# Gated linear-scan mixer with a routed feed-forward: batch loop written out, a fifth plane added by DMA, small work moved in the engines' orders

## Chip, cores and metric

The kernel runs on one core of a Trainium2 chip. The metric is device time of one execution in microseconds. Before the change three runs took 678.12, 679.08 and 682.12 us; the median is 679.08 us. The five engines of the core each run a program of their own and meet only at semaphores: PE (TensorE: matrix products and transposes), DVE (VectorE), ACT (ScalarE), POOL (GpSimd) and SP (SyncE, which here only issues DMAs). POOL issues DMAs too.

## What is computed

The input x is 8 batches of 1024 tokens of 256 features. In short:

```python
x = x + layernorm(attn(layernorm(x)))
x = x + layernorm(ffn(layernorm(x)))

# attn: 4 mixers m, each token weighs its best two
g, v, d = z @ Wg[m] + bg[m], z @ Wv[m] + bv[m], z @ Wd[m] + bd[m]
a = 0.001 + 0.998 * sigmoid(d)
h[t] = a[t] * h[t-1] + sigmoid(g[t]) * tanh(v[t])     # scan along the 1024 tokens
attn = sum over m of comb[:, m] * h_m                  # comb: softmax of the two best gate logits

# ffn: each batch is sent to one of 8 experts
z = layernorm(x) * ln_g + ln_b
probs = softmax(batchnorm(mean over tokens of z) @ Wr + br); e = argmax(probs)
ffn = (relu(z @ W_down[e] + b_down[e]) @ W_up[e] + b_up[e]) * probs[e]
```

## The kernel before, in words

**Tiling.** A batch is 1024 tokens. The mixers work on the transposed batch (features on partitions): 4 mixers times 2 halves of 128 features give 8 *planes* of 128 x 1024. A plane needs three projections (gate, decay, value) for two chunks of 512 tokens, so a batch has 48 *products*, numbered i = 0 to 47 in the code (plane i // 6). One product is 6 matmuls of 128 x 512 (weights and input are each split into a high and a low half-precision part; three of the four cross terms, over two halves of the contraction). Three PSUM banks take turns, so product i waits until ACT has read product i-3 (`main_read`). ACT's `evacuate` applies the sigmoid or tanh and writes the plane to one of four slots (`gate_s`, `decay_s`) or to `hid`.

**DVE's part of a plane** is `multiply` (gate times value, L932), `scan` (L914) and `weigh` (times the token's weight of that mixer, L926).

**Sum over mixers.** Plane p and plane p+2 are the same features of successive mixers. POOL's `add_plane(p)` (L486) is a DMA that adds plane p to plane p+2 in SBUF; it is issued for p = 0 to 3, one after the other, so that planes 4 and 5 hold the sum of three mixers. PE's `turn_plane` (L1389) then transposes planes 4, 5, 6, 7 (`TURNED`) back to token rows, 8 transposes of 128 x 128 each, and sums what is left in PSUM (`ps_aux`, seen by tokens as `ps_tok`).

**What follows the sum, for the batch before (`pv`), while the products of the present batch run:** on DVE `a_moments` (statistics of the turned rows), `residual`, `t_moments`, `scale_t`; on ACT `normalise_t` (L640); on PE `turn_u` (L1326); on ACT `high_u`; on PE `route`; on DVE `low_u` (L959), `route_logits`, `route_pick` (L978); SP reads the expert's index and copies its weights (`load_expert`); on PE `down` (L1448); `high_h`, `low_h`, PE's `up`; on DVE `y_moments`, `scale_y` (L1015); on ACT `scale_rows` (L663, eight rows, in pairs ahead of products 43 to 46); on DVE `finish` (L1022, adds the residual) and SP's `store`.

**For the batch after (`nx`):** `x_moments`, `normalise_x`, `high_rows_x` and `low_rows_x` (split), two DMA transposes by SP (`move_x`, L400, which wait for `plane_added[1]`), PE's `gates`, DVE's `rank_mixers`, ACT's `shares`, DVE's `weights_of` (`comb`), PE's `turn_weights` (L1354), DVE's `copy_weights` (L904), and SP's saving and loading of the weights (`save_comb`, `load_comb`).

**Order.** There is no scheduler. Each engine's program is written by hand: PE and ACT in three functions (`run_first`, `run`, `last`) that walk over the 48 products and put other work ahead of a given i; DVE in a list of calls per batch. `iterations` (L232) runs batch 0 as `run_first`, batches 1 to 6 in a loop of the hardware with two batches in its body (three passes), and batch 7 as `last`, which cuts the batch into two chunks. An engine does its work strictly in its order, so a wait holds up all that is written behind it.

**First batch.** SP loads weights; ACT casts each weight matrix to its high part (`high_matrix`, L537), DVE makes the low part (`low_matrix`, L830). `hidden_bias` (L1489, L1492) are 33 narrow matmuls ahead of product 15 that need `prepare_router` (ends in L1085) and other constants. Some `prepare_` calls on DVE ready the experts' weights.

## Time and profile before

| | |
|---|---|
| profiled execution, time | 678.97 us |
| its span, first to last instruction | 677.2 us |
| PE busy | 618.5 us, 91% |
| DVE busy | 587.4 us, 87% |
| ACT busy | 461.1 us, 68% |
| POOL busy | 99.7 us, 15% |
| mean granted clock of PE | 0.974 |

Matmuls are pipelined; a row's duration is longer than the step from one to the next (a 128 x 512 matmul shows 0.38 us and the next begins 0.216 us later at full clock, so that a product steps by 1.296 us). In a timeline row the first number is the start in us from the start of the span, the second the duration (of the whole merged group where the count behind the x is above 1), and the bracket tells how long the engine sat idle before it and what ended that.

### The profile page before, as it was taken

What the parts mean: (1) busy time and instruction counts of PE and PEld (TensorE: products, weight loads), DVE (VectorE), ACT (ScalarE), POOL (GpSimd) and SP (SyncE); (2) the same over time, 40 slices, a digit from 0 to 9 for tenths busy, and PEclk for the clock granted to TensorE, in tenths of its full rate; (3) what the DMA queues carried; (4) which work ended last, traced back from release to release, by engine and by line L of the source; (5) the groups of instructions that cost most, each with busy time, mean ns of one, the idle gap of its engine ahead of it and who ended that gap; (6) DMA issues with size and microseconds to landing.
All of it is one profiled execution on the core that took longest, in us unless ns stands there. A gap on an engine that the chain in (4) does not pass through costs nothing. (4 is left out here: it accounts for less than half of the span.)

```text
span 677.2 us, 10435 instructions
## 1 busy us (share of the span) xinstructions
PE 618.5 (91%) x3314; PEld 318.4 (47%) x3314; DVE 587.4 (87%) x1094; ACT 461.1 (68%) x791; POOL 99.7 (15%) x101
## 2 busy tenths in 40 slices
PE   3989999999999989999998989999998999899673
PEld 2454454445545535445544535445544554444431
DVE  6799599999899987999899987999899988889866
ACT  3728655896579675896579675896669775877404
POOL 2002011302121101302121101202030102112011
PEclk9979999999999999999999999999999999999687
DMA  8651736154712736054621737045631735211003
GB/s 224 153 187 32 156 62 237 26 111 78 253 60 54 141 101 219 1 106 93 233 80 43 144 100 228 0 96 104 209 104 43 130 99 179 44 31 32 0 22 115
DMA packets 74627, 73.27 MB, mean 108 GB/s; under 512 B 36134, under 2 KB 66122, under 8 KB 74570
## 3 DMA queue, kind: packets, MB, share of 16 engines
q1 hardware_dynamic: 69676, 56.30, 28.8%
q0 software_dynamic: 4896, 16.26, 12.9%
q8 instruction: 32, 0.52, 0.3%
q14 instruction: 23, 0.19, 0.1%
HBM read 38.85 MB, written 8.52 MB: 70 GB/s over the span
## 5 line engine op out<-in xcount | busy, mean ns | idle before, releaser
L1375 PE MATMUL ps_main<-xh,w_hi 128*128 128x512 f16 x768 | 292.5, 381 | 6.9 <-issue 5.7
L1375 PE MATMUL ps_main<-xh,w_lo 128*128 128x512 f16 x768 | 292.4, 381 | 0.0
L1375 PE MATMUL ps_main<-xl,w_hi 128*128 128x512 f16 x768 | 292.3, 381 | 0.0
L914 DVE TENSOR_TENSOR_SCAN hid<-decay_s,hid 128x1024 f32<-128x1024 f32 (+1 forms) x64 | 138.2, 2159 | 6.6
L581 ACT ACTIVATE hid<-ps_main,vecs 128x512 f32<-128x512 f32 x128 | 88.9, 695 | 60.5 <-PE ps_main L1375 60.1
L581 ACT ACTIVATE decay_s<-ps_main,vecs 128x512 f32<-128x512 f32 x128 | 88.9, 695 | 59.1 <-PE ps_main L1375 57.9
L1375 PEld LDWEIGHTS ps_main<-xh,w_hi 128*128 128x128 f16 x768 | 76.1, 99 | 94.6 <-issue 7.8
L581 ACT ACTIVATE gate_s<-ps_main,vecs 128x512 f32<-128x512 f32 x128 | 88.6, 692 | 44.8 <-PE ps_main L1375 43.8
L1375 PEld LDWEIGHTS ps_main<-xl,w_hi 128*128 128x128 f16 x768 | 75.4, 98 | 91.6 <-issue 1.7
L1375 PEld LDWEIGHTS ps_main<-xh,w_lo 128*128 128x128 f16 x768 | 75.3, 98 | 85.7 <-issue 1.1
L932 DVE TENSOR_TENSOR hid<-gate_s,hid 128x1024 f32<-128x1024 f32 (+1 forms) x72 | 79.5, 1105 | 6.5 <-ACT hid L581 6.0
L926 DVE TENSOR_TENSOR hid<-hid,comb_all 128x1024 f32<-128x1024 f32 (+1 forms) x72 | 79.7, 1107 | 2.8
L587 ACT ACTIVATE decay_s<-decay_s 128x1024 f32<-128x1024 f32 (+1 forms) x72 | 69.6, 967 | 0.0
L486 POOL DMA_DIRECT2D hid<-hid x34 | 30.0, 882 | 245.6 <-DVE hid L926 170.8
L468 POOL TENSOR_TENSOR root_a<-root_in_a,neg_half 128x8 f32<-128x8 f32 (+1 forms) x9 | 19.0, 2111 | 151.8 <-DVE root_in_a L816 151.8
L1326 PE MATMUL ps_aux<-ident,normed 128*128 128x128 f32 x136 | 19.5, 302 | 23.4 <-ACT normed L640 13.2
L1389 PE MATMUL ps_aux<-ident,hid 128*128 128x128 f32 x264 | 32.9, 285 | 3.3 <-DVE hid L926 2.2
L1389 PEld LDWEIGHTS ps_aux<-ident,hid 128*128 128x128 f32 x264 | 31.3, 148 | 5.8 <-DVE hid L926 2.8
L640 ACT ACTIVATE normed<-resid,shift_t,root_t 128x256 f32<-128x256 f32 x60 | 30.5, 595 | 4.2 <-DVE shift_t L823 4.2
L594 ACT ACTIVATE u_split<-ps_aux 128x512 f16<-128x512 f32 x32 | 18.9, 600 | 19.0 <-PE ps_aux L1411 17.7
L808 DVE BATCH_NORM_STATS2 stats_a<-ps_aux 128x6 f32<-128x256 f32 x64 | 22.1, 419 | 10.5 <-PE ps_aux L1389 10.5
L1326 PEld LDWEIGHTS ps_aux<-ident,normed 128*128 128x128 f32 x136 | 16.9, 155 | 27.8 <-ACT normed L640 17.1
(152 smaller groups left out, 606.9 us busy)
## 6 DMA issues: line engine op xcount, KB each, us to landing
comb_all<-comb_dram SPq DMA_DIRECT2D x32, 512.0 KB, 5.1
hid<-hid POOLq DMA_DIRECT2D x28, 512.0 KB, 4.6
x_in<-in_L_attn_x SPq DMA_DIRECT2D x16, 512.0 KB, 7.5
resid<-in_L_attn_x SPq DMA_DIRECT2D x8, 1024.0 KB, 6.1
out<-resid SPq DMA_DIRECT2D x7, 1024.0 KB, 5.5
expert<-experts SPq DMA_DIRECT2D x8, 192.5 KB, 2.2
hid<-hid POOLq DMA_DIRECT2D x6, 256.0 KB, 3.3
w_stage<-in_L_attn_Wg SPq DMA_DIRECT2D x4, 256.0 KB, 3.9
```

The costliest lines, as they stand in the source:

```text
L468: pool.tensor_tensor(root[key][:, span(c)], root_in[key][:, span(c)], neg_half[:, span(c)], ALU.pow).then_inc(rooted, units(c))
L486: pool.dma_start(hid[:, p + KT, tokens(c)], hid[:, p, tokens(c)], accum_op=ALU.add).then_inc(plane_added[p], 16)
L581: act.activation(dst, ps_main[:, i % BANKS], ACT.Tanh if kind == VALUE else ACT.Sigmoid, bias=vecs[:, col:col + 1], scale=Q_W).then_inc(ma ...
L587: act.activation(d, d, ACT.Copy, bias=0.001, scale=0.998).then_inc(decay_ready, 1)
L640: ins = act.activation(out[:, t], rows[:, t], ACT.Identity, bias=shift[key][:, t:t + 1], scale=root[key][:, t:t + 1])
L808: ins = dve.bn_stats(out=stats[key][:, t], in_=rows(t))
L914: dve.tensor_tensor_scan(states(pc), staged(decay_s, pc, pc.c), states(pc), start, ALU.mult, ALU.add).then_inc(scanned, 1)
L926: dve.tensor_tensor(src, src, comb_all[:, m, tokens(pc.c)], ALU.mult).then_inc(weighed, 1)
L932: dve.tensor_tensor(v, staged(gate_s, pc, pc.c), v, ALU.mult).then_inc(input_ready, 1)
L1326: ins = pe.transpose(ps_aux[:, KT * cc + k, tile(t % (T // C))], normed[:, t, k * P:(k + 1) * P], ident[:])
L1375: ins = pe.matmul(ps_main[:, i % BANKS], w[:, 3 * m + kind, k, half * P:(half + 1) * P], v[:, bt.par, span(c), k], start=(n == 0), stop=(n ...
L1389: ins = pe.matmul(ps_tok[:, t, k * P:(k + 1) * P], hid[:, p, tile(t)], ident[:], is_transpose=True, start=(p == (LATE_TURNED if c else TUR ...
```

## The change

The hardware loop goes: `iterations` now calls `run` six times, with batch numbers known when the program is built. POOL issues a fifth addition, plane 4 to plane 6, and PE turns only planes 5, 6 and 7; it does so one product later (i = 5). Small work changes its place. In steady batches: PE turns the weights ahead of product 45 and not behind 47; ACT's `shares` stands ahead of product 43, before the wait for `y_scaled`, and not ahead of 44; on DVE `weights_of` moves ahead of plane 6, `finish` and then `copy_weights` stand between plane 6 and plane 7, and `route_logits` stands before `low_u`. In the first batch ACT, DVE and PE take the casts, splits, gates and preparations in another order.

```diff
-    TURNED = (4, 5, 6, 7)
+    TURNED = (5, 6, 7)
...
-        def iterations(eng, run_first, run, last):
+        def iterations(run_first, run, last):
...
-            with eng.Fori(0, B // 2 - 1) as j:
-                for r in (1, 2):
-                    run(turn(j, r), turn(j, r + 1), turn(j, r - 1))
+            for n in range(1, B - 1):
+                run(turn(n // 2, n % 2), turn((n + 1) // 2, (n + 1) % 2), turn((n - 1) // 2, (n - 1) % 2))
...
# POOL, run
                 power("y", y_root_in, y_root, pv)
+                add_plane(bt, 4)
# POOL, last
                 add_plane(bt, 3, 0)
+                add_plane(bt, 4, 0)
...
# ACT, run_first
+                        high_matrix(0, VALUE)
                         high_x(bt, 0)
-                        high_matrix(0, VALUE)
+                    if i == 1:
+                        high_gate_weights()
                         mixer_high(1)
                         high_x(bt, 1)
-                    if i == 3:
-                        high_gate_weights()
+                    if i == 4:
+                        mixer_high(2)
                     if i == 6:
-                        mixer_high(2)
-                    if i == 7:
+                        mixer_high(3)
+                    if i == 9:
                         shares(bt)
-                        mixer_high(3)
-                    if i == 21:
+                    if i == 25:
                         normalise_x(nx, tiles(0))
-                    if i == 25:
+                    if i == 26:
                         normalise_x(nx, tiles(1))
...
# ACT, run
                     if i == 23:
                         normalise_x(nx, tiles(0))
-                    if i == 24:
                         router_sigmoids(pv)
...
                     if i == 43:
+                        shares(nx)
                         act.wait_ge(xh_moved, 16 * nx.n)
                         act.wait_ge(xl_moved, 16 * nx.n)
                         act.wait_ge(y_scaled, pv.n + 1)
                         scale_rows(pv, (0, 1), normed)
                     if i == 44:
-                        shares(nx)
                         scale_rows(pv, (2, 3), normed)
...
# DVE, ahead of the first batch
             x_moments(first, 0)
+            scale_x(first, 0)
+            normalise("x", x_in, x_scaled, x_normed, first, 0)
             low_matrix(0, GATE)
-            scale_x(first, 0)
             low_matrix(0, DECAY)
-            normalise("x", x_in, x_scaled, x_normed, first, 0)
+            low_matrix(0, VALUE)
             x_moments(first, 1)
+            copy_vecs()
             low_x(first, 0)
-            copy_vecs()
-            low_matrix(0, VALUE)
...
# DVE, run_first
                 mixer_low(1)
+                prepare_router(prep)
+                mixer_low(2)
+                rank_mixers(bt)
                 set_ones()
-                rank_mixers(bt)
                 weights_of(bt)
-                mixer_low(2)
-                mixer_low(3)
                 copy_weights(bt, True)
-                prepare_up_biases(prep)
-                prepare_router(prep)
                 prepare_down(prep, 0)
                 multiply(bt, pcs[0])
...
# DVE, run
+                route_logits(pv)
                 low_u(pv)
-                route_logits(pv)
                 route_pick(pv)
...
                 scale_y(pv)
+                weights_of(nx)
                 multiply(bt, pcs[6])
                 scan(bt, pcs[6])
                 weigh(bt, pcs[6])
-                weights_of(nx)
+                finish(pv)
                 copy_weights(nx, False)
                 multiply(bt, pcs[7])
                 scan(bt, pcs[7])
                 weigh(bt, pcs[7])
-                finish(pv)
...
# PE, run_first
-                    if i == 5:
+                    if i == 3:
                         first_gates(bt)
-                    if i == 8:
+                    if i == 11:
                         turn_weights(bt)
...
# PE, run
-                    if i == 4:
-                        turn_planes(pv, (4, 5, 6, 7))
+                    if i == 5:
+                        turn_planes(pv, (5, 6, 7))
...
+                    if i == 45:
+                        turn_weights(nx)
                     product(bt, i, bank, False)
-                turn_weights(nx)
```

The engines' orders at the places that matter. First PE, from the end of the loop's body: the rows before show the turning of the weights, the jump back to the loop's start, and (word for word the first rows behind it) the next product.

```order
L1354 MATMUL ps_misc<-ident,comb 32x128 [waits comb_ready]
L238 REGISTER_ALU
L238 COMPARE_AND_BRANCH
L1375 MATMUL ps_main<-xh,w_hi 128x512 [waits main_read,xl_moved,xh_moved]
L1375 MATMUL ps_main<-xh,w_lo 128x512
```

In the program after the change no L238 row stands on PE at all; the weights' transpose has moved three products up. The turning of the planes in a steady batch, with the names of the semaphores that each plane waits for (`plane_added4` is the new addition), now reads:

```order
L1391 MATMUL ps_aux<-ident,hid 128x128 [waits plane_added3,weighed,y_normed]
L1391 MATMUL ps_aux<-ident,hid 128x128 x7
L1391 MATMUL ps_aux<-ident,hid 128x128 [waits plane_added4,weighed]
L1391 MATMUL ps_aux<-ident,hid 128x128 x7
L1391 MATMUL ps_aux<-ident,hid 128x128 [waits weighed]
L1391 MATMUL ps_aux<-ident,hid 128x128 x7
```

Before, four such pairs stood there, the first for plane 4. On DVE the end of a steady batch, from `scale_y` to the first statistics of the next batch, read before:

```order
L1015 TENSOR_TENSOR shift_y<-shift_y,shift_a 128x8 [waits out_link]
L930 REGISTER_ALU
L932 TENSOR_TENSOR hid<-gate_s,hid 128x1024 [waits main_read]
L914 SCALAR_TENSOR_TENSOR hid<-decay_s,hid 128x1024 [waits input_ready,decay_ready]
L926 TENSOR_TENSOR hid<-hid,comb_all 128x1024 [waits comb_loaded3,scanned]
L897 TENSOR_TENSOR comb<-share,chosen 128x8x4 [waits share_ready]
L904 COPY comb_rows<-ps_misc 32x128 [waits comb_saved,comb_turned]
L930 REGISTER_ALU
L932 TENSOR_TENSOR hid<-gate_s,hid 128x1024 [waits main_read]
L914 SCALAR_TENSOR_TENSOR hid<-decay_s,hid 128x1024 [waits input_ready,decay_ready]
L926 TENSOR_TENSOR hid<-hid,comb_all 128x1024 [waits scanned]
L1022 TENSOR_TENSOR resid<-normed,resid 128x2048 [waits y_normed]
```

After the change the same stretch of DVE is (line numbers are two higher):

```order
L1017 TENSOR_TENSOR shift_y<-shift_y,shift_a 128x8 [waits out_link]
L899 TENSOR_TENSOR comb<-share,chosen 128x8x4 [waits share_ready]
L934 TENSOR_TENSOR hid<-gate_s,hid 128x1024 [waits main_read]
L916 SCALAR_TENSOR_TENSOR hid<-decay_s,hid 128x1024 [waits input_ready,decay_ready]
L928 TENSOR_TENSOR hid<-hid,comb_all 128x1024 [waits comb_loaded3,scanned]
L1024 TENSOR_TENSOR resid<-normed,resid 128x2048 [waits y_normed]
L906 COPY comb_rows<-ps_misc 32x128 [waits comb_saved,comb_turned]
L934 TENSOR_TENSOR hid<-gate_s,hid 128x1024 [waits main_read]
L916 SCALAR_TENSOR_TENSOR hid<-decay_s,hid 128x1024 [waits input_ready,decay_ready]
L928 TENSOR_TENSOR hid<-hid,comb_all 128x1024 [waits scanned]
```

The weights' product has moved ahead of plane 6, where it waits for ACT's `share`, and the addition of the residual ahead of plane 7, where it waits for all of ACT's scaled rows.

## Rows read from the trace of the kernel before

**Rows 1.** The page, part 1: busy us (share of the span) and instructions by engine.

```profile
PE 618.5 (91%) x3314; PEld 318.4 (47%) x3314; DVE 587.4 (87%) x1094; ACT 461.1 (68%) x791; POOL 99.7 (15%) x101
```

**Rows 2.** Timeline of PE: the weights' transposes that end batches 1 and 6.

```profile
169.81 0.27 PE L1354 MATMUL ps_misc<-ident,comb 128*32 128x128 f32 x1
...
551.56 0.27 PE L1354 MATMUL ps_misc<-ident,comb 128*32 128x128 f32 x1
```

**Rows 3.** Busy time by stretch (start:end length, engines, clock, DMA): batches 2 and 3.

```profile
170.00:245.10 75.10, 73.22 (x402) 37.16 (x400) 68.81 (x121) 56.75 (x98) 11.96 (x8) 1.00 0.44 116
245.10:323.30 78.20, 73.43 (x404) 37.45 (x403) 68.84 (x121) 56.91 (x99) 11.96 (x8) 1.00 0.44 111
```

**Rows 4.** Waits in batch 3 (engine, line, what ended it: us, times, longest).

```profile
PE ps_main L1375 <- issue: 2.8, 1, 2.8
```

**Rows 5.** Timeline, start of batch 2: plane 7 weighed, planes turned, residual added.

```profile
174.82 1.23 DVE L926 TENSOR_TENSOR hid<-hid,comb_all 128x1024 f32<-128x1024 f32 x1
175.10 3.66 PE L1389 MATMUL ps_aux<-ident,hid 128*128 128x128 f32 x32
175.96 2.28 DVE L1022 TENSOR_TENSOR resid<-normed,resid 128x2048 f32<-128x2048 f32 x1
```

**Rows 6.** Timeline, batch 2: from DVE's scale to ACT's rows and PE's transposes.

```profile
197.76 0.17 DVE L823 SCALAR_TENSOR_TENSOR shift_t<-moments_t,root_t 128x8 f32<-128x8 f32 x1
...
199.03 1.09 ACT L640 ACTIVATE normed<-resid,shift_t,root_t 128x256 f32<-128x256 f32 x2
...
203.13 1.97 PE L1326 MATMUL ps_aux<-ident,normed 128*128 128x128 f32 x16 [1.07 <-ACT normed L640]
```

**Rows 7.** Timeline, batch 2: low parts, router and expert.

```profile
207.53 2.48 DVE L959 TENSOR_TENSOR u_split<-ps_aux,u_split 128x512 f16<-128x512 f32 x4
...
211.70 0.20 DVE L978 RECIPROCAL r<-r 128x8 f32<-128x8 f32 x1 [0.64 <-ACT r L600]
...
214.76 1.90 PE L1448 MATMUL ps_aux<-u_split,expert 128*128 128x512 f16 x8 [0.32 <-DMA expert<-experts]
```

**Rows 8.** Timeline, end of batch 2: scale, first and last scaled rows, plane 6.

```profile
238.87 0.17 DVE L1015 TENSOR_TENSOR shift_y<-shift_y,shift_a 128x8 f32<-128x8 f32 x1
...
239.48 1.02 ACT L663 ACTIVATE normed<-ps_aux,shift_y,root_y 128x256 f32<-128x256 f32 x2
...
242.62 1.23 DVE L926 TENSOR_TENSOR hid<-hid,comb_all 128x1024 f32<-128x1024 f32 x1
...
244.02 1.08 ACT L663 ACTIVATE normed<-ps_aux,shift_y,root_y 128x256 f32<-128x256 f32 x2
```

**Rows 9.** Timeline: an addition's issue, and SP's transpose that waits for it.

```profile
217.89 0.86 POOL L486 DMA_DIRECT2D hid<-hid  x1 [8.77 <-DVE hid L926]
...
223.11 1.76 SPq L400 DMA_TRANSPOSE xh<-normed  x1
```

**Rows 10.** POOL's line of the 34 additions: time from issue to landing.

```profile
DMA to landing us min/median/max: 3.2/4.5/6.4
```

**Rows 11.** Timeline, first batch on PE, ACT and DVE.

```profile
26.84 1.66 ACT L537 ACTIVATE w_hi<-w_stage 128x512 f16<-128x512 f32 x3
...
29.33 3.69 DVE L830 SCALAR_TENSOR_TENSOR w_lo<-w_stage,w_hi 128x512 f16<-128x512 f32 x6
29.49 0.29 PE L1354 MATMUL ps_misc<-ident,comb 128*32 128x128 f32 x1 [1.64 <-DVE comb L897]
...
40.94 0.36 PE L1489 MATMUL ps_misc<-z_wr,ones 128*128 128x8 f32 x2 [2.10 <-DVE z_wr L1085]
...
47.49 0.59 PE L1375 MATMUL ps_main<-xh,w_hi 128*128 128x512 f16 x1
```

**Rows 12.** Busy time by stretch in the narrow matmuls: clock is the last but two.

```profile
41.80:42.20 0.40, 0.40 (x4) 0.40 (x3) 0.40 (x2) 0.00 (x0) 0.00 (x0) 0.50 1.03 341
```

**Rows 13.** Timeline of PE: the last planes of batch 0, turned in batch 1.

```profile
102.33 1.09 PE L1389 MATMUL ps_aux<-ident,hid 128*128 128x128 f32 x8 [0.99 <-DVE hid L926]
```

**Rows 14.** Timeline of PE, last batch: the wait for ACT's rows.

```profile
579.23 0.98 PE L1326 MATMUL ps_aux<-ident,normed 128*128 128x128 f32 x7 [3.19 <-ACT normed L640]
```

More of the change, by code:

```diff
@@ L193, in mixer_kernel @@
         weighed = sem("weighed")
-        plane_added = [sem(f"plane_added{p}") for p in range(4)]
+        plane_added = [sem(f"plane_added{p}") for p in range(5)]
         add_go = sem("add_go")
@@ L441, in last @@
                 sp.wait_ge(out_stored, 16 * (B + 2 * C) + 1)
-            iterations(sp, run_first, run, last)
+            iterations(run_first, run, last)
         @block.gpsimd
@@ L526, in last @@
                 power("y", y_root_in, y_root, bt, 1)
-            iterations(pool, run_first, run, last)
+            iterations(run_first, run, last)
         @block.scalar
@@ L782, in last @@
                 scale_late_rows(bt, 1)
-            iterations(act, run_first, run, last)
+            iterations(run_first, run, last)
         @block.vector
@@ L1314, in last @@
                 finish_late(bt, 1)
-            iterations(dve, run_first, run, last)
+            iterations(run_first, run, last)
         @block.tensor
@@ L1567, in last @@
                 up(bt, 1)
[L1569 removed]
+            iterations(run_first, run, last)
 _INS = ["L0_attn_x", "L0_attn_Wg", "L0_attn_bg", "L0_attn_Wv", "L0_attn_bv", "L0_attn_Wd", "L0_attn_bd",
```

28 lines of the change are left out of this document (15 added, 13 removed).

## Prediction, made before the changed kernel ran

> **What bounds the kernel now.** I read the page's busy times first, then the trace batch by batch. PE is busy for 618.5 of 677.2 us, DVE for 587.4 [rows 1]: both are close to the bound, and a share of the whole cannot say which sets the pace. The transposes of the weights close each batch on PE and serve as a clock: batch 1 closes at 169.81, batch 6 at 551.56 [rows 2]. By stretch, batch 2 lasts 75.10 us and batch 3 lasts 78.20 with the same work [rows 3]; batch 4 repeats the one and batch 5 the other. Inside 75.1 us PE is busy for 73.2 and DVE for 68.8: **in a steady batch PE sets the pace, and DVE has a few us of slack**. The long batches are the two that begin behind a jump back of the loop, and there PE waits 2.8 us at a product for "issue", that is for nothing that a semaphore shows [rows 4].
>
> I measure inside a steady batch from the end of PE's turning of the planes, T. In batch 2 that is 175.10 + 3.66 = 178.76 [rows 5].
>
> **The change, part by part.**
>
> *Loop written out.* The two jumps back go. Each costs 78.2 - 75.1 = 3.1 us [rows 3], and since PE is the bound the whole of it goes: **-6.2**. Below that the gain is nothing if written-out code brings stalls of its own. Batches 1 and 2 are code run for the first time, in a straight line, and show no such wait in 75.1 us [rows 3], so I take the full price.
> The Trainium skill, "Runtime: NRT & Kernel Launch", section "Instruction fetch mechanics", says that straight code is fetched ahead and that a taken branch out of the fetched window stalls. The trace agrees, with 2.8 us.
>
> *Three planes turned, not four.* 32 transposes take 3.66 us [rows 5], so eight fewer are **-0.92** per batch on PE.
>
> *The turning one product later.* PE loses nothing by it, but DVE's chain behind it starts later against the products. That chain ends with `scale_t` at 197.93, T + 19.17; ACT takes it up at 199.03, 1.10 later, because it came there only then, by the products [rows 6]. A product steps by 1.296 us, so now one product fewer lies between T and ACT's arrival: ACT is 1.30 earlier, uses up the 1.10 and waits 0.20. PE's wait at the transposes grows from 1.07 by that: **+0.20**.
>
> *`route_logits` before `low_u`.* The index is known 2.48 us earlier [rows 7], DVE's wait of 0.64 for the sigmoids is covered by `low_u`, and PE's wait of 0.32 for the expert's weights goes: **-0.35** (0.3 to 0.5 over the batches).
>
> A steady batch so takes 75.1 - 0.92 + 0.20 - 0.35 = 74.05 us.
>
> *Can DVE follow?* `scale_y` ended at 239.04, T + 60.28. PE and ACT now are 1.3 + 0.35 - 0.20 = 1.45 earlier against T. Two waits are new. `weights_of` waits for ACT's `share`; ACT, which began its rows at 239.48, now comes at T + 59.3 and is held until `scale_y`. `finish` waits for all eight rows, 5.6 us of ACT's time (239.48 to 245.10), and then takes 2.28 [rows 5] ahead of plane 7, which takes 4.8 like plane 6 (239.04 to 243.85) [rows 8]. If DVE is no earlier than before, rows end at T + 65.9, `finish` at 68.2, plane 7 at 73.3. If it keeps the 0.64 and some smaller waits it is rid of, about 1.1 earlier, plane 7 is weighed at T + 72.2. PE reaches plane 7 at T + 74.05 - 0.92 = 73.1. So the price is 0 to 0.2 per batch; I take 0, as the waits that go are rows and the later case needs them all to stay. `copy_weights`, now behind `finish`, hands the weights over 2 us later; they are needed only behind the next batch's first scan, after T, so this is hidden. `turn_weights` at product 45 comes 1.4 us behind `weights_of`: no wait. What is queued behind a late `finish` is plane 7, then PE's turning.
>
> *The fifth addition.* No row shows plane 4's addition. The nearest is an addition of the same size, issued at 217.89 (POOL issues some 0.6 us after the plane is weighed) and waited for by SP until 223.11, 5.2 us [rows 9]; all 34 land within 3.2 to 6.4 us [rows 10]. Plane 6 is weighed at T + 64.5 to 65.1, so the sum lands at T + 70.3 by the nearest row, 72.1 by the slowest; PE reaches plane 6 at T + 72.2. Cost 0. Behind it on POOL stands only the root for the next batch's `a_moments`, which comes after T.
>
> *First batch.* The split of the first chunk now comes behind one more split and the copy of the vectors, and a split lost its cover (POOL's root): two splits of 0.61 (3.69 / 6) and a small copy make **+1.5** on the first product [rows 11]. The gates stand two products earlier and need the second chunk, which ACT casts only behind three weight matrices (1.66, of which PE's other work covers half): product 5 falls behind by 2.3 in all. But the two waits of PE, 1.64 and 2.10, go, since router and weights are prepared earlier. Product 15, at 47.49 [rows 11], so comes at 46.05: 2.3 - 3.74 = -1.44. Two blocks of four normalisations (two take 1.09, rows 6) now stand one product apart, and PE's three banks cover 0.75 less than that: +0.75. In batch 1 PE waited 0.99 for plane 7 of batch 0 [rows 13]; DVE, with less of its preparation ahead of that plane, is earlier there and the wait goes, and plane 4 with it (0.92). With the steady terms that batch 1 has too (-0.35 + 0.20): -1.44 + 0.75 - 0.99 - 0.92 - 0.15 = **-2.75** at the close of batch 1. These steps go by order and durations and may be off by 2 either way.
>
> *Clock.* PE stood idle for 2.10 us ahead of the narrow matmuls [rows 11], and 0.9 us into them the granted clock had fallen to 0.50, its lower level (1.2 GHz) [rows 12]; so of their 6.55 us (40.94 to 47.49) 0.9 ran at the upper level and 5.65 at the lower. Now the wide matmuls run right up to them. If the clock falls as they begin, nothing is gained; if all of them run at the upper level they take (2 x 0.9 + 5.65) / 2 = 3.7, 2.8 less. Not all of that lasts: `gates` may then wait for the transposed next batch, and plane 6's sum for its DMA. Bounds 0 and -2.8; I take about half, **-1.3**.
>
> *Last batch.* PE waits 3.19 for rows that hang on DVE's chain [rows 14], so fewer transposes there gain nothing. DVE starts that chain at nearly the same distance from the close of batch 6, by the steps above: +0.1.
>
> **Sum**, against the profiled execution's 678.97 us (its span 677.2; 0.1 from the median of 679.08): -6.2 (loop) - 5.25 (batches 2 to 6, 5 x 1.05) - 2.75 (to the close of batch 1) - 1.3 (clock) + 0.1 = -15.4, **663.6 us**.
>
> **Rivals.**
> *DVE becomes the bound.* For: 68.8 of 75.1 us busy, plus the two new waits; the batch shrinks to 74.05. Against: the waits that go are as long. If plane 7 comes 1 us late in each batch, 6 us come back: 669.
> *Straight code stalls too.* Every engine fetches four more batches of code. Against: batches 1 and 2. If it gives the 6.2 back: 669.
> *The first batch loses.* If one of the old waits stays (router or expert preparation, 2.1) and the clock falls all the same: 678.97 - 15.4 + 2.1 + 1.3 = 667.
> *The clock stays up altogether*: 1.5 more from the narrow matmuls, and the products behind them, which step at half rate at first, lose nothing either (some 2): 660.
> *The other side: the fifth addition holds PE.* PE does nothing else while it waits at plane 6, so all products and with them ACT and DVE stand. It costs from a landing 7.1 us after plane 6 is weighed, and turns the change into a loss when it is 15.4 / 7 = 2.2 us later still, a landing of 8.7 us from the issue, in each batch: at 9 us 681. Against: no landing above 6.4 [rows 10].
> The Trainium skill, "SBUF — State Buffer", section "SBUF: two separate sides", speaks for it: a DMA issued from POOL needs POOL's cores to write descriptors, and a VectorE copy in a two-port mode locks them out. The trace does not bear it out: the addition at 217.89 was issued under a DVE operation and took 0.86 [rows 9]. By the rule, `finish` (2.28) could hold the new issue, and the sum would land at about T + 72.6, 0.4 late per batch: 666, inside the forecast's range; I give it 0.05 of the forecast's 0.57.
>
> **How the numbers follow.** Forecast 0.57 (661 to 666.5); DVE bound 0.14; straight code stalls 0.09; first batch loses 0.09; clock up 0.06; addition late 0.05. A measurement of this kernel tells about 1% from no change, 6.8 us. All but the last lie below 672.3; of DVE's and the code's cases I count a third as worse than their price, within 1%. Faster 0.85, within 1% 0.10, slower 0.05. Range 657 to 670: it takes in both clock bounds and the rivals at 667 and 669, and leaves out late additions and the worse thirds.
>
> **What would show it.** In the changed trace: closes of batches 74 us apart, all alike, no wait for "issue" on PE; 24 transposes of 2.75 us a batch without a wait inside; PE's wait at the u transposes 1.07 to 1.3; no wait for the expert's DMA; DVE waiting about 0.4 at `comb` and 0.4 at `finish`, and 1 to 2 for the planes; product 15 at about 43 to 46. Wrong if the closes stay 75 apart (then see who waits ahead of plane 6 or 7), if PE shows waits for issue elsewhere, or if product 15 starts later than 47.5.

## The result and the profile after

The changed kernel takes 663.78 us (median of 4 runs, 661.74 to 665.05) and the kernel before, beside it, 678.6 (median of 4): a ratio of 0.975, 95% interval 0.970 to 0.980. The forecast was 663.6. The profiled execution took 664.04 us with a span of 662.2, against 678.97 and 677.2 before: 15.0 us of span are gone, where the forecast's sum had 15.4.

Page, part 1, of the changed kernel: busy us (share of the span) and instructions, to set beside [rows 1].

```profile
PE 608.8 (92%) x3254; PEld 308.1 (47%) x3254; DVE 585.2 (88%) x1094; ACT 459.8 (69%) x791; POOL 105.2 (16%) x109
```

PE has 60 transposes fewer (7 turnings x 8, and 4 in the half batch at the end) and 9.7 us less to do; POOL has eight more (8 issues of additions, 5.5 us).

The timeline's transposes of the weights are the clock of the batches, as in [rows 2]. The first line closes batch 0, where nothing of the batch follows it. In batches 1 to 6 they now stand ahead of product 45, so three products (3.89 us) of the batch still follow.

```profile
89.37 0.27 PE L1356 MATMUL ps_misc<-ident,comb 128*32 128x128 f32 x1
159.69 0.27 PE L1356 MATMUL ps_misc<-ident,comb 128*32 128x128 f32 x1
234.26 0.27 PE L1356 MATMUL ps_misc<-ident,comb 128*32 128x128 f32 x1
308.48 0.27 PE L1356 MATMUL ps_misc<-ident,comb 128*32 128x128 f32 x1
382.71 0.27 PE L1356 MATMUL ps_misc<-ident,comb 128*32 128x128 f32 x1
456.91 0.27 PE L1356 MATMUL ps_misc<-ident,comb 128*32 128x128 f32 x1
531.51 0.27 PE L1356 MATMUL ps_misc<-ident,comb 128*32 128x128 f32 x1
```

From the second line on the distances are 74.57, 74.22, 74.23, 74.20 and 74.60 us. No batch is 3 us longer than its neighbours any more. With the three products added, batch 1 ends at 163.70 (before: 169.93) and batch 6 at 535.52 (551.68):

| stretch | forecast | measured |
|---|---|---|
| to the end of batch 1 | -4.05 (2.75 work and waits, 1.3 clock) | 163.70 - 169.93 = -6.23 |
| batches 2 to 6 | -11.45 (6.2 jumps, 5.25 the rest) | 371.82 - 381.75 = -9.93 |
| last batch and tail | +0.1 | 126.68 - 125.52 = +1.16 |
| span | -15.4 | -15.0 |

So the total came out within half a us, but by three misses that cancel (2.2 better, 1.5 worse, 1.1 worse): that closeness is luck.

Busy time by stretch, batches 2 and 3 of the changed kernel (start:end, length, PE, PEld, DVE, ACT, POOL, clock, DMA), the counterpart of [rows 3]:

```profile
163.70:238.30 74.60, 72.46 (x395) 36.34 (x394) 68.50 (x121) 56.65 (x99) 12.80 (x9) 1.00 0.49 123
238.30:312.50 74.20, 72.41 (x395) 36.33 (x394) 68.51 (x121) 56.59 (x98) 12.80 (x9) 1.00 0.50 124
```

The waits of PE inside batch 3, where [rows 4] had 2.8 us for "issue" (engine, line, what ended it: us, times, longest):

```profile
PE ps_aux L1328 <- ACT normed L642: 1.2, 1, 1.2
PE ps_misc L1438 <- ACT u_split L596: 0.6, 1, 0.6
```

And the timeline at the end of batch 2 and the start of batch 3, to set beside [rows 5, 8]:

```profile
232.93 0.21 DVE L899 TENSOR_TENSOR comb<-share,chosen 128x32 f32<-128x32 f32 x1 [0.58 <-ACT share L557]
...
238.38 2.29 DVE L1024 TENSOR_TENSOR resid<-normed,resid 128x2048 f32<-128x2048 f32 x1 [0.46 <-ACT normed L665]
238.52 0.92 POOL L485 DMA_DIRECT2D hid<-hid  x1 [7.10 <-DVE hid L928]
...
244.42 1.23 DVE L928 TENSOR_TENSOR hid<-hid,comb_all 128x1024 f32<-128x1024 f32 x1
244.73 2.78 PE L1391 MATMUL ps_aux<-ident,hid 128*128 128x128 f32 x24
...
247.55 2.75 DVE L810 BATCH_NORM_STATS2 stats_a<-ps_aux 128x6 f32<-128x256 f32 x8 [1.91 <-PE ps_aux L1391]
```

The 24 transposes run through in 2.78 us without a wait inside: plane 7 is weighed at 245.65, 0.93 before PE comes to it (244.73 + 2 x 0.93), and the fifth addition has landed. The issue of that addition lay wholly under DVE's `finish` (238.38 to 240.67) and took 0.92, in the 0.86 to 1.05 of all 42 issues, so this operation did not hold POOL up. DVE waits 0.6 at `comb`, 0.5 at `finish` and 1.9 for the planes, much as the forecast listed. One wait put down to issue is new on PE, 2.92 us ahead of its very first product (14.79); that product needs the low split of x, which DVE ends at 14.69, and the wait is there with the loop too, so it is no price of the straight code.

### The profile page after: what moved, and what is told of

It reads as the page before. It is cut to its first block and busy times, and to the rows that moved or that the text cites. A ratio compares the mean times of both kernels' runs of the same rounds, so it can differ in the third digit from the quotient of the medians.

```text
span 662.2 us, 9326 instructions
## 1 busy us (share of the span) xinstructions
PE 608.8 (92%) x3254; PEld 308.1 (47%) x3254; DVE 585.2 (88%) x1094; ACT 459.8 (69%) x791; POOL 105.2 (16%) x109
## 5 line engine op out<-in xcount | busy, mean ns | idle before, releaser
L485 POOL DMA_DIRECT2D hid<-hid x42 | 37.1, 884 | 284.7 <-DVE hid L928 212.7
L1391 PE MATMUL ps_aux<-ident,hid 128*128 128x128 f32 x204 | 26.0, 284 | 4.4 <-DVE hid L928 2.9
L642 ACT ACTIVATE x_in<-x_in,shift_x,root_x 128x256 f32<-128x256 f32 x56 | 29.1, 606 | 0.0
```

The source lines that it names most:

```text
L485: pool.dma_start(hid[:, p + KT, tokens(c)], hid[:, p, tokens(c)], accum_op=ALU.add).then_inc(plane_added[p], 16)
L642: ins = act.activation(out[:, t], rows[:, t], ACT.Identity, bias=shift[key][:, t:t + 1], scale=root[key][:, t:t + 1])
L1391: ins = pe.matmul(ps_tok[:, t, k * P:(k + 1) * P], hid[:, p, tile(t)], ident[:], is_transpose=True, start=(p == (LATE_TURNED if c else TUR ...
```

## The experiments

All twelve are complete kernels, each timed beside the kernel before, and the ratios are taken from that pair. The medians of the kernel before were 684.36 us beside the first four, 679.95 beside the next four (late addition, router, swap, split halves) and 678.79 to 679.0 beside the rest: they scatter by 0.8%, so for differences of a few us between kernels I read the closes of the batches, in one profile of each. The kernels with the changed first batch close batch 0 at 89.2 to 91.1 us, so a difference under 2 us in that stretch alone tells nothing.

### The loop written out

The kernel before, with one edit (`e1_straight_only`), and the changed kernel with the loop back (`e2_loop_kept`):

```diff
-            with eng.Fori(0, B // 2 - 1) as j:
-                for r in (1, 2):
-                    run(turn(j, r), turn(j, r + 1), turn(j, r - 1))
+            for n in range(1, B - 1):
+                run(turn(n // 2, n % 2), turn((n + 1) // 2, (n + 1) % 2), turn((n - 1) // 2, (n - 1) % 2))
```

> The kernel before with one edit, the loop of two batches written out. Theory (the jump back costs TensorE 2.8 us after batch 2 and 3.1 after batch 4, and nothing hides them): both waits put down to issue are gone, the closes of batches 3 and 5 move 3 us nearer, about 672.5 us, 0.9909 of before. Rival (straight code is fetched at a price of its own): waits put down to issue appear in other batches and the time stays near 678.5, 1.000. The profile decides between them: the distance of the closes in batches 2 to 6 is 75.1 in all of them by the theory.

Measured: 673.25 us (ratio 0.986, 0.979 to 0.993). The medians say 11.1 us less than the kernel before beside it, the profiles 6.5 of span; the closes are the surer measure. The closes of the kernel before were 76.54, 75.13, 78.18, 75.08, 78.29 and 75.07 apart; now it is 76.19, 75.27, 74.98, 74.98, 74.98 and 75.21. The two long batches lost 3.20 and 3.31 us, and no wait for issue came up on PE in its steady batches. The waits of its batches 2 to 6:

```profile
PE ps_aux L1325 <- ACT normed L639: 5.2, 5, 1.0
PE ps_misc L1435 <- ACT u_split L593: 2.9, 5, 0.6
PE ps_aux L1447 <- DMA expert<-experts: 0.8, 2, 0.4
```

Two things more are to be read here. The wait for the expert's weights, which the change was forecast to remove by another edit, is gone from batches 3 to 5 by the straight code alone; the 0.8 us are 0.4 in each of batches 2 and 6. And these two batches are 0.2 to 0.3 longer than the others. They are 0.25 to 0.4 longer in every other kernel without the loop but the one with the late addition, where larger waits cover it. The timeline of the changed kernel shows the place, one instruction of DVE in batch 2:

```profile
176.56 0.17 DVE L817 SCALAR_TENSOR_TENSOR moments_a<-moments_a 128x8 f32<-128x8 f32 x1 [0.46 <-DVE moments_a L816]
```

Elsewhere this step follows its predecessor without such a gap. In all twelve straight kernels DVE pauses by 0.3 to 0.5 us at the same three instructions, in batches 2, 3 and 6; in the two kernels with the loop it does not pause there. Straight code is thus not quite free: about 0.35 us in each of two batches of the changed kernel reaches PE, 0.7 us. The place speaks for the fetching of code. The trace lists transfers of the kind "instruction": 26 of 16 KB on queue q8 and 22 of 8 KB on q14 within the changed kernel's span. PE's 6600 recorded instructions (matmuls, weight loads and its sequencer's) fit the 26, at some 64.5 bytes each; by that estimate a block of 8 KB holds 127. The three pauses stand at DVE's recorded instructions number 320, 577 and 961, 257 and 384 apart, which is two and three such blocks to within 3 instructions. Why only these three block ends pause is open, and no such transfer falls into a pause itself.

> The changed kernel with the loop of two batches put back and everything else as in it. Theory: two waits of 2.8 to 3.1 us put down to issue come back on TensorE, 664 + 6 = 670 us. Rival: with the transpose of the weights now ahead of product 45, the jump falls in among products and lies partly beside the evacuations still to be done, so that less than 3 us of the 6 come back: under 667 us.

Measured: 670.67 us (0.982, 0.975 to 0.988). The median says 6.9 more than the changed kernel, the profile 6.1 of span, of which 1.7 lies in the first batch, where the code is the same. The loop itself costs less: the closes are 74.22, 76.13, 74.22, 76.31 and 74.26 apart, so a jump now costs 1.9 to 2.1 us, and the profile puts its wait down to ACT (the second is 1.80 us, at 392.22).

```profile
241.70 0.39 PE L1378 MATMUL ps_main<-xh,w_hi 128*128 128x512 f16 x1 [1.63 <-ACT hid L584]
```

The rival was right that the jump is partly covered, but not on the size: of the 6.5 us that the loop cost before, 4.0 come back here (less the 0.7 of straight code, 3.3), not under 3, and 670.67 is nearer the theory's 670 than the rival's 667.

What is covered can be read from the transfers of code. Queue q8 at the first jump, in the kernel before (DMA of 245.1 to 245.2 us), then here (238.75 to 238.85):

```profile
q8 instruction: 1, 0.02, 70.3%
```

```profile
q8 instruction: 1, 0.02, 72.8%
```

Before, such a transfer starts at 245.15, 0.1 us behind the close of the batch (245.05), and PE's next product at 248.02; here it starts at 238.80, 1.1 us ahead of the close (239.91), and the next product at 241.70. At the second jump it is 398.41 and 401.39 before, 389.19 and 392.22 here. So in all four cases PE goes on 2.9 to 3.0 us after a transfer of code has started. With the loop kept in the new order that transfer starts while products are still to run, and the 1.2 us by which it is earlier against the close match the 1.2 to 1.3 us that the jump costs less. In `e1_straight_only` no such transfer starts within 6 us of these two closes.

### The fifth addition and the three planes

```diff
-    TURNED = (5, 6, 7)
+    TURNED = (4, 5, 6, 7)
...
-                add_plane(bt, 4)
...
-                        turn_planes(pv, (5, 6, 7))
+                        turn_planes(pv, (4, 5, 6, 7))
```

> The changed kernel without the fifth addition, so that plane 4 is turned on TensorE again (32 transposes in place of 24, at the same place in the order). Theory: each of the seven turnings takes 3.66 us in place of 2.78, the half of the last batch 0.46 more, all of it on TensorE's path: 664 + 6 = 670 us, steady period 75.1 in place of 74.2. Rival: the steady period is set by ScalarE and VectorE around the turning of u, whose wait of 1.15 us on TensorE shrinks by what the turning grows: 664 to 665 us, steady period 74.2 to 74.4.

Measured: 668.75 us (0.978, 0.972 to 0.984). Closes 75.43, 75.08, 75.08, 75.08 and 75.46 apart, +0.85 to 0.88 in each batch, and 5.0 us by the close of the last. The turning of batch 4 starts as the forecast's unit of account has it:

```profile
321.39 3.66 PE L1388 MATMUL ps_aux<-ident,hid 128*128 128x128 f32 x32
```

3.66 - 2.78 = 0.88 is what each batch lost: a transpose saved on the bound engine is saved whole. The waits behind it (1.14 for u, 0.58 at the route) did not shrink. The last batch and tail did not grow (126.6 us against 126.7), so the theory's 0.46 there did not show: four planes cost it nothing. And against the kernel before with straight code (74.98), the period of 75.08 shows what all the other edits of the steady batch, the loop apart, are worth together: nothing, 0.1 us worse.

### The first batch

The changed kernel with the first batch's order and preparation of before on DVE, ACT and PE; of the lines:

```diff
-            scale_x(first, 0)
-            normalise("x", x_in, x_scaled, x_normed, first, 0)
             low_matrix(0, GATE)
+            scale_x(first, 0)
...
-                prepare_router(prep)
-                mixer_low(2)
                 rank_mixers(bt)
...
+                prepare_up_biases(prep)
+                prepare_router(prep)
```

> The changed kernel with the order of the first batch (and of the preparation ahead of it) of before on VectorE, ScalarE and TensorE; loop, additions and steady batches as changed. Theory A (what the forecast had summed for the first batch, 1.8 us of work and waits and 1.3 us of clock): 664 + 3 = 667 us. Theory B (the clock is worth more, 2.5 us in the narrow matmuls and a further 2 in the products behind them): 664 + 5 = 669 us, with the narrow matmuls at 6.5 us and a granted clock of 0.50 until about 50 us. Which one it is shows at the close of batch 0: 91.5 or 93.5 us.

Measured: 668.98 us (0.979, 0.973 to 0.985). Batch 0 closes at 93.80, 4.4 later than in the changed kernel, and the granted clock stands at 0.50 from 42.2 to 52.5: theory B. By the close of batch 1 the loss is 6.45, for a reason that I had not listed:

```profile
98.62 0.87 POOL L485 DMA_DIRECT2D hid<-hid  x1 [4.02 <-DVE hid L927]
...
103.24 1.94 PE L1390 MATMUL ps_aux<-ident,hid 128*128 128x128 f32 x16 [1.82 <-DMA hid<-hid]
```

DVE weighs plane 6 of batch 0 late in the old order, the new addition is issued late by as much, lands 4.5 us behind (the median of all landings is 4.6), and PE waits 1.82 for it. The new addition needs the new first batch.

To take the clock apart from the waits, one piece of the preparation alone was put later (`e7_router_late`):

```diff
                 mixer_low(1)
-                prepare_router(prep)
...
                 scan(bt, pcs[0])
+                prepare_router(prep)
                 weigh(bt, pcs[0])
```

> The changed kernel with one edit: the router's preparation on VectorE stands between the scan and the weighing of the first plane, so that z_wr is ready about 41 us and TensorE sits idle for about 2 us ahead of the narrow matmuls, as it did before. Theory (the fall of the clock starts earlier or later with the idle ahead of it): the narrow matmuls take 6.5 us in place of 4.0, the clock stays at 0.50 until about 50 us, and product 15 starts at about 47.5 in place of 42.9. Rival (the narrow matmuls bring the fall by themselves): they take 4.0 us again, product 15 starts at 45.0, and the clock is back by 48. The close of batch 0 is 4.5 us later by the first, 2 us by the second.

Measured: 668.41 us (0.981, 0.976 to 0.986). The narrow matmuls, first in the changed kernel (the first two, the other 32, and product 15 behind them), then in this one:

```profile
38.86 0.28 PE L1491 MATMUL ps_misc<-z_wr,ones 128*128 128x8 f32 x2
...
39.00 4.02 PE L1494 MATMUL ps_misc<-vecs,u_split 128*128 128x1 f32 x32
42.88 0.59 PE L1377 MATMUL ps_main<-xh,w_hi 128*128 128x512 f16 x1
```

```profile
41.96 0.36 PE L1491 MATMUL ps_misc<-z_wr,ones 128*128 128x8 f32 x2 [2.95 <-DVE z_wr L1087]
...
48.16 0.59 PE L1377 MATMUL ps_main<-xh,w_hi 128*128 128x512 f16 x1
```

Busy time by stretch of the changed kernel in and behind the narrow matmuls (clock last but two), and of this one:

```profile
40.00:41.90 1.90, 1.90 (x19) 1.90 (x19) 1.87 (x2) 0.00 (x0) 0.00 (x0) 1.00 1.02 395
...
42.30:45.60 3.30, 3.30 (x11) 1.59 (x11) 3.27 (x2) 0.00 (x0) 0.00 (x0) 0.50 0.99 340
45.80:48.00 2.20, 2.20 (x12) 1.02 (x11) 2.17 (x7) 1.21 (x2) 0.00 (x0) 1.00 0.01 5
```

```profile
43.20:53.20 10.00, 10.00 (x37) 6.73 (x37) 9.26 (x17) 0.69 (x1) 0.00 (x0) 0.50 0.37 126
53.40:56.00 2.60, 2.60 (x14) 1.18 (x12) 2.29 (x7) 1.90 (x3) 1.67 (x1) 1.00 0.00 0
```

With an idle of 2.95 us ahead, the same matmuls take 6.20 in place of 4.02, and the lower level (0.50, 1.2 GHz) lasts into the products until past 53, some 10 us; without an idle it sets in only 3.4 us into them and is over by 45.7. Product 15 comes 5.28 later: 3.10 by its later start and 2.18 by the slower matmuls. Batch 0 closes 5.94 later, so an idle of 2.95 us cost about twice its length, give or take the 2 us by which this stretch scatters.

The other profiles bear the two courses out, with a reserve. All four kernels with an idle of 2.1 to 2.95 us there show 10.2 us at 0.50. Of the ten without it eight show 3.4 us, the one with `down` at 29 shows 6.8 (0.50 from 42.2 to 48.9), and the one with the loop kept no fall there but 3.4 us at 78.6. Those last two are the ones that close batch 0 at 91.1. So the idle brings the long course; how short the other is, and when it comes, is not settled by it.

### The swap of route_logits and low_u

```diff
-                route_logits(pv)
                 low_u(pv)
+                route_logits(pv)
```

> The changed kernel with one edit: in the steady batches VectorE does the low part of u ahead of the routing's logits again. The forecast's step gave the swap 0.35 us in each batch (the wait for the expert's weights at the down product): undone, that is +0.35 x 6 = 2.1, about 666 us, and waits of 0.3 to 0.5 us for the expert come back at the down product. Rival, from the two earlier runs (steady period 74.98 with the loop alone written out, 75.08 with all of the change but the plane): the swap gives next to nothing, 664 to 664.5 us, and what it gained comes back at the wait for u.

Measured: 670.86 us (0.987, 0.981 to 0.992); period 75.41, +1.2 a batch. Both expectations were wrong. The timeline of batch 3:

```profile
282.28 0.21 ACT L601 ACTIVATE r<-r 128x8 f32<-128x8 f32 x1 [1.70 <-DVE r L970]
283.21 0.39 PE L1377 MATMUL ps_main<-xh,w_hi 128*128 128x512 f16 x1 [0.66 <-ACT hid L583]
```

ACT's sigmoids, which the change has moved from product 24 to 23, wait 1.70 for the logits; ACT evacuates nothing meanwhile, and PE waits 0.66 at a product, which so starts 0.8 late; the next one is 0.2 late again. The waits for the expert came back too, but only in two batches (0.25 and 0.16). The swap is worth 1.2 us a batch against its own partner, the sigmoids' new place, while all the other edits of the steady batch together are worth nothing (75.08 against 74.98): an edit undone alone prices the pair, not the edit. What swap and sigmoids are worth together was not run.

### A late fifth addition

```diff
-                pool.wait_ge(weighed, PLANES * bt.n + PLANES * (c or 0) + p + 3)
+                pool.wait_ge(weighed, PLANES * bt.n + PLANES * (c or 0) + (8 if p == 4 else p + 3))
```

> The changed kernel with one edit: the fifth addition waits for the last plane (7) to be weighed and not for plane 6, so that it is issued about 7 us later. Theory (the addition's landing has to stand ahead of the turning, and has 5 us of slack now): the landing comes 3 to 5 us after the turning of plane 6 could begin, in each of six turnings, 664 + 18 to 30 = 682 to 694 us, slower than the kernel before, with waits for the DMA on TensorE at plane 6. Rival: TensorE's and VectorE's slack behind the turning (VectorE waits 1.9 us for it) takes most of it, under 675 us.

Measured: 746.9 us (1.097, 1.091 to 1.104), far above even the theory. PE waits 71.6 us for additions, 9.4 to 12.3 in each of seven turnings. Timeline of POOL, PE and SP's queue around one:

```profile
266.54 3.65 SPq L315 DMA_DIRECT2D comb_all<-comb_dram  x4
270.24 0.43 SPq L341 DMA_DIRECT2D out<-resid  x1
270.45 0.92 POOL L485 DMA_DIRECT2D hid<-hid  x1 [14.83 <-DVE hid L928]
270.71 5.72 SPq L301 DMA_DIRECT2D x_in<-in_L_attn_x  x2
...
279.47 3.43 PE L1391 MATMUL ps_aux<-ident,hid 128*128 128x128 f32 x16 [9.50 <-DMA hid<-hid]
```

The addition, issued one plane later, falls in among the loads of the weights, the store of 1 MB and the loads of x that SP issues from 266.5 on, and PE goes on 9.0 us after its issue (the seven late ones land in 8.8 to 10.4), where the changed kernel's additions land within 3.3 to 6.4. That these loads and stores slow it is likely by the times, not tested by itself. The cliff that the prediction's rival named is there, and steeper than its 681 us. The loss of 83 us is more than the waits: in each of these waits the granted clock falls to 0.50 and stays there for 10 to 14 us (272.3 to 282.5 in the batch shown), and over the whole run it is 0.935 in place of 0.983.

### PE's last waits in the steady batch

Three kernels tried to take the waits of 1.15 (u) and 0.58 (route) away, in steps that build on each other. The first splits ACT's normalising around an evacuation:

```diff
                     if i == 19:
                         normalise_t(pv, tiles(0))
+                    if i == 20:
                         normalise_t(pv, tiles(1))
...
-                    if i == 22:
+                    if i == 23:
                         turn_u(pv)
-                    if i == 23:
+                    if i == 24:
                         route(pv)
```

> The changed kernel with one edit in the steady batches: ScalarE normalises the two halves of t at products 19 and 20 (before: both at 19), with an evacuation between them, and TensorE turns u one product later (23), the route behind it (24). Theory: TensorE's wait of 1.15 us for normed is there because ScalarE does 4.0 us of normalising while TensorE has only three buffers, 3.9 us of products, to go on with; with an evacuation between there are four, so the wait goes: 664 - 1.15 x 6 = 657 us. Rival: everything behind u comes one product later, and the wait returns at the route, at the down product or at the closing finish: 663 to 665 us.

Measured: 663.6 us (0.976, 0.970 to 0.981), period 74.0. The wait for u falls to 0.44, and the one for the expert comes back:

```profile
270.74 1.97 PE L1329 MATMUL ps_aux<-ident,normed 128*128 128x128 f32 x16 [0.44 <-ACT normed L642]
...
281.45 1.90 PE L1451 MATMUL ps_aux<-u_split,expert 128*128 128x512 f16 x8 [0.64 <-DMA expert<-experts]
```

Then `down` at product 29 with ACT's parts behind it:

```diff
-                    if i == 28:
+                    if i == 29:
                         down(pv)
```

> The kernel with the halves of t split, and the down product one product later (29) with ScalarE's hidden parts and splits of h behind it (29, 30, 32, 33). Theory: the wait of 0.6 us for the expert's weights that took the place of the wait for u goes, steady period 73.4 in place of 74.0, about 659.5 us. Rival (VectorE is next to bind, with only 3 us of waits left in a period): VectorE waits for h by up to 1.3 us, the weighing of plane 7 comes later, and TensorE waits for it at the turning: period 74.0 or more.

Measured: 663.9 us (0.977, 0.972 to 0.981), period 74.17 to 74.27. The waits of DVE in one steady batch:

```profile
DVE stats_a L812 <- PE ps_aux L1393: 1.3, 1, 1.3
DVE h L991 <- ACT h L607: 0.8, 1, 0.8
DVE resid L1026 <- ACT normed L665: 0.7, 1, 0.7
```

PE's wait for the expert is gone, and DVE waits 0.8 for h instead. Last, `route` at 25, the sigmoids at 24, `down` at 30:

```diff
-                    if i == 24:
+                    if i == 25:
                         route(pv)
...
-                    if i == 29:
+                    if i == 30:
                         down(pv)
```

> As that, with the route two products behind u (25) and ScalarE's sigmoids at 24, the down product at 30, hidden parts 30 and 31, splits of h 33 and 34. Theory: the wait of 0.58 us for u_split at the route goes as well, period 72.8, about 655 us. Rival (VectorE binds): the logits wait on VectorE, h comes 2.6 us later than in the changed kernel, and TensorE waits at the turning of the planes, at up or for products' evacuation: period 74 to 75, 664 to 670 us.

Measured: 667.01 us (0.981, 0.977 to 0.986), period 74.7 to 74.8. The longest waits of PE in one steady batch:

```profile
PE ps_aux L1478 <- DVE up_in L1004: 0.8, 1, 0.8
PE ps_aux L1331 <- ACT normed L642: 0.4, 1, 0.4
```

The wait at the route is gone and stands at `up`, behind DVE; two products wait 0.2 each for ACT. The rivals' times were right three times, and their mechanism twice: with `down` at 29 PE's listed waits shrink from 1.7 to 1.2 us a batch, it never waits for plane 7 at the turning, and the period is 74.2 all the same, so where the gain went is not shown. There are 72.4 us of work on PE and 68.5 on DVE in a batch, and none of the places tried is better by more than 0.2 us.

### The last batch

Turnings of planes and u and ACT's normalising one product later each, in the last batch alone:

```diff
-                    if i == 3:
+                    if i == 4:
                         turn_planes(pv, (5, 6, 7))
-                    if i == 16:
+                    if i == 17:
                         turn_u(pv)
```

> The changed kernel with edits in the last batch alone: the three planes are turned one product later (4), ScalarE normalises t one product later (14), TensorE turns u one product later (17), ScalarE splits it one product later (17). Theory: the turning ends when it did, since it ends on plane 7's weighing, and one product (1.3 us) now lies inside its waits of 0.31 and 1.15 us; the turning of u again waits about 2.2 us: from the close of batch 7 to the last turning of six planes 1.3 us less than the changed kernel's, about 662.5 us. Rival: ScalarE's normalising, one product later, holds the turning of u back by what was gained, 664 us. On the clock: it fell at this turning of u in five of ten profiles so far (route 7.4 us behind the start of the turning in place of 5.7) with waits ahead of it of 2.2 to 2.8 us, and not in five others with waits of 1.0 to 3.2; if the idle's length decides, it falls again with 2.2 and not with 1.0.

Measured: 663.55 us (0.976, 0.971 to 0.980). From the last transposes of the weights (531.42) to the first turning of six planes (601.86) 70.44 us pass in place of 71.73, the 1.3 of the theory; at the end of the span 0.5 of it is left. The rest goes on PE in the tail, at the last route (changed kernel, then this one) and the products behind it:

```profile
640.92 0.58 PE L1422 MATMUL ps_misc<-wr_mul,u_sums 128*128 128x8 f32 x4 [1.12 <-ACT u_split L596]
```

```profile
639.54 0.99 PE L1422 MATMUL ps_misc<-wr_mul,u_sums 128*128 128x8 f32 x4 [1.12 <-ACT u_split L596]
```

The route still starts 1.38 earlier, but in these 0.58 us the granted clock is 1.00 and in these 0.99 it is 0.50; the next products (L1463) take 3.59 in place of 3.22, at 0.52 and 0.58. So the lower clock takes 0.8 of the gain back; ScalarE's normalising, which the rival had doing it, does not. The clock fell again at the turning of u, with the same wait as in the changed kernel:

```profile
562.98 2.48 PE L1328 MATMUL ps_aux<-ident,normed 128*128 128x128 f32 x16 [2.19 <-ACT normed L642]
...
564.00:567.50 3.50, 3.50 (x15) 2.07 (x14) 3.27 (x6) 3.46 (x11) 0.92 (x1) 0.54 0.03 6
```

With the split halves of t beside it:

> The changed kernel with the halves of t split in the steady batches (period 74.0 in place of 74.2) and the last batch's turnings one product later. Theory: the two gains add, 0.2 x 6 + 1.3 = 2.5 us, about 661.3 us and a span of 658.8 (659.7 if the clock falls at the last batch's turning of u, less 1.7 if not). Rival: the last batch's gain is given back by its tail, as it was for the most part in the run with the last batch's edits alone (0.5 us of 1.3 was left): 662.3 us.

Measured: 662.38 us (0.974, 0.969 to 0.979), span 660.1, periods 74.3 and 74.0. It is the lowest of all, 1.4 us under the changed kernel, but the two were not timed beside each other and their runs overlap (659.95 to 664.08 against 661.74 to 665.05): not told apart.

## Why the prediction was right, and where its steps were not

**What bounds the kernel** held. PE sets the pace in the steady batch: 0.88 us taken off it was 0.86 off the period, and DVE's two new waits cost nothing, as argued.

**Loop: right on its own, not additive.** -6.2 was forecast; written out alone it gave 6.5 in the two batches. In the changed kernel the same jumps would have cost 4.0, since the transfer of code there starts 1.1 us ahead of the batch's close. The straight code also has a small price of its own, 0.7, which I had at nothing because batches 1 and 2 of the kernel before showed no wait on PE; the pauses are DVE's, and come in batches 2, 3 and 6 of code written out. The Trainium skill, "Runtime: NRT & Kernel Launch", section "Instruction fetch mechanics", has sequential fetch as mostly hidden; the 0.3 to 0.5 us at three instructions of DVE agree with "mostly", if they are that.

**Steady batch: 74.05 forecast, 74.2 measured, with 74.6 twice.** The planes came as forecast (-0.92; 0.86 to 0.88). The mis-sized term is the swap: the -0.35 for the expert's wait was read from the loop's batches, and in straight code that wait is gone from the undisturbed batches (75.1 falls to 74.98 there, by 0.1 only), so nothing was left to win. The +0.20 of the later turning measured +0.11 (1.04 in straight code to 1.15). The rest of the edits is neutral. Over five batches, 5 x 0.17 and the 0.7 of straight code make the 1.5 us.

**First batch: 4.05 forecast, 6.2 measured.** The work and the waits were about right in sum; the clock was mis-sized. I took 1.3, half of an upper bound of 2.8 for the narrow matmuls, and gave the products behind them nothing in the forecast. The matmuls went from 6.55 to 4.02 us (2.5), and the lower level behind them lasted 2.8 us in place of 4.4, 0.8 more by the half rate: 3.3, some 2.0 above the term, which is the miss. The stretch scatters by up to 2 us between kernels with the same first batch, so the rows of the clock carry this reading, and not the 6.2. Both pieces stood in the rival "the clock stays up altogether", which had 0.06; what happened lies between the forecast and that rival. The run with the idle put back shows that the idle brings the long fall.

**Last batch: +0.1 forecast, +1.16 measured.** From the turning of u to the route 7.37 us passed in place of 5.68, 1.69 more, at a granted clock of 0.57. No edit explains it. In 14 profiles of these kernels the clock fell there in seven, with waits of 2.15 to 2.80 us ahead, and not in the seven others, with waits of 1.01 to 3.19; four kernels show the same 2.2 and no fall. What decides it stays open. Four kernels with the same last batch and no fall there (old first batch, swap undone, router late, `down` at 29) take 124.8 to 125.6 us for this stretch, against 125.5 before: without the fall the forecast's +0.1 would have been about right (-0.7 to +0.1). The changed kernel's rows, the counterpart of [rows 14], and the stretch between them:

```profile
563.07 2.37 PE L1328 MATMUL ps_aux<-ident,normed 128*128 128x128 f32 x16 [2.20 <-ACT normed L642]
...
570.44 0.95 PE L1438 MATMUL ps_misc<-wr_mul,u_sums 128*128 128x8 f32 x8
```

```profile
564.00:567.50 3.50, 3.50 (x16) 2.06 (x15) 3.29 (x6) 3.50 (x11) 0.92 (x1) 0.57 0.00 0
```

**The fifth addition** cost nothing, as forecast, with 0.92 us for an issue wholly under `finish`. The passage of the Trainium skill that I weighed ("SBUF — State Buffer", section "SBUF: two separate sides") has POOL locked out while VectorE runs an operation in a two-port mode, such as an fp32 copy. `finish` is an operation on two tensors, like the one over the issue at 217.89: I stretched the passage to them, and these rows do not test it for a copy. The rival's threshold was about right: I had PE at plane 6 7.1 us after it is weighed, and in the run with the late addition it comes there at 7.9 (weighed at 262.12, wait from 269.97). What failed is the argument against it, "no landing above 6.4": that holds for the place of issue that the kernel has. One plane later the same addition lands in 8.8 to 10.4, and 83 us are lost where the forecast's case, with 9 us from the old place, had 17.

## What to carry to other kernels

A saving on the engine that sets the pace counts whole, but here savings elsewhere (a shorter chain, an earlier handover) were worth only the wait that was left with the other edits in; read that wait from a trace with them in, or expect the gain to move. Edits come in pairs: before undoing or taking over one, look for the instruction on another engine that was moved to suit it. An idle of PE ahead of many narrow matmuls cost about twice its length here, so bring forward the small work that it waits for. And a new transfer should be issued ahead of the next burst on the queues: one plane later cost 83 us here, a cliff and not a slope.

## What the runs showed of the hardware

- An idle of 2 to 3 us ahead of the narrow matmuls brought the granted clock down to 0.50 for 10.2 us in four profiles of four (41.7 to 51.9 before, 43.1 to 53.3 with the router late); of ten without it, eight show 3.4 us, one 6.8, and one no fall there.
- The same idle of 2.2 us ahead of 16 transposes and full products brought a fall in the profiles of five kernels (2.15 to 2.20) and none in four others (2.19 to 2.20).
- A jump back cost PE 3.2 to 3.3 us in the kernel before and 1.9 to 2.1 where products stood on both sides of the last handover of the batch. PE's next product started 2.9 to 3.0 us after a 16 KB transfer of code had started, at all four jumps.
- DVE pauses 0.3 to 0.5 us at three fixed instructions of the straight code, 257 and 384 instructions apart, in twelve kernels of twelve.
- An accumulating transfer of 512 KB inside SBUF lands in 4.6 us at the median, and in 8.8 to 10.4 when issued among 4 MB of other loads and stores.
